# Quantising the first layer's weights ahead of the feed-forward block, and turning its inputs by DMA

## What is computed

```python
# x: 8 x 512 x 1024, context: 8 x 512 x 1024, 64 heads of 8 rows, L = 1024
kv  = einsum('bhil,bhjl->bijhl', ctx, ctx)             # per head 8 x 8 products
out = causal_convolution(kv, ssm_kernel) + kv * D      # along l, for each head
out = einsum('bijhl,bhil->bjhl', out, layernorm(x))
x   = x + tanh(g_xattn) * out                          # the "mixer"
h = bf16(layernorm_weighted(bf16(layernorm(x))))
h = bf16(mx_quant(h) @ mx_quant(W1).T + b1)            # W1: 4096 x 1024
h = bf16(gelu_tanh(h))
h = bf16(mx_quant(h) @ mx_quant(W2).T + b2)            # W2: 1024 x 4096
x = x + tanh(g_ffn) * bf16(residual + h)
# mx_quant: blocks of 32 along the contraction share the power of two of their largest magnitude;
# values are rounded to integers on that scale and clipped to -128..127
```

## Time and profile before

| | |
|---|---|
| median of three runs | 2044.43 us |
| the profiled execution itself | 2045.5 us |
| its span in the trace | 2043.7 us |
| PE busy | 1931.1 us (94%) |
| DVE busy | 1735.5 us (85%) |
| POOL busy | 967.6 us (47%, nearly all of it in the mixer) |
| ACT busy | 735.7 us (36%) |

### The profile page before, as it was taken

The page is one execution under the profiler, slowest core; times in us unless marked ns, Lnnn a source line. Parts: engine busy times, 40 slices in busy tenths (PEclk is TensorE's granted clock), DMA queues, the critical chain, the costliest instruction groups (busy, mean ns, idle before and its releaser), DMA issues. The chain is left out here.

```text
span 2043.7 us, 29510 instructions
## 1 busy us (share of the span) xinstructions
PE 1931.1 (94%) x11776; PEld 1488.6 (73%) x11776; DVE 1735.5 (85%) x2092; ACT 735.7 (36%) x1028; POOL 967.6 (47%) x1036
## 2 busy tenths in 40 slices
PE   6999999999999999999826599999999999999998
PEld 5888888888788888888725466677776666667763
DVE  6888898898899999999779979888888888888843
ACT  3232222222222222222126444545544444455540
POOL 3888888888899999999912000000000000000000
PEclk9999999999999999999958799999999999999999
DMA  6555555555354555544437401111111111111111
GB/s 220 188 201 195 195 192 195 196 200 211 127 181 175 182 174 177 190 165 168 164 124 278 166 31 51 43 63 63 63 63 63 42 52 63 63 42 52 42 42 73
DMA packets 65769, 264.40 MB, mean 129 GB/s; under 512 B 7712, under 2 KB 7712, under 8 KB 57440
## 3 DMA queue, kind: packets, MB, share of 16 engines
q1 hardware_dynamic: 65632, 262.52, 36.1%
HBM read 219.96 MB, written 42.53 MB: 128 GB/s over the span
## 5 line engine op out<-in xcount | busy, mean ns | idle before, releaser
L242 PE MATMUL y_ps<-kk_hi,slab 128*128 128x512 f32 (+8 forms) x3072 | 872.9, 367 | 9.3 <-DMA slab<-taps_scratch 5.2
L242 PEld LDWEIGHTS y_ps<-kk_hi,slab 128*128 128x128 f32 x3072 | 559.2, 189 | 106.3 <-DMA slab<-taps_scratch 5.6
L242 PE MATMUL y_ps<-kk_lo,slab 128*128 128x512 f32 (+8 forms) x1536 | 563.0, 367 | 0.0
L714 PE MATMUL l_ps<-f_xq_T,w_T 128*128 128x256 bf16 x4096 | 461.4, 276 | 16.3 <-ACT arena L793 13.6
L714 PEld LDWEIGHTS l_ps<-f_xq_T,w_T 128*128 128x128 bf16 x4096 | 404.7, 99 | 70.3 <-ACT arena L793 13.9
L729 PE MATMUL acc_ps<-w_T,arena 128*128 128x512 bf16 x2048 | 449.0, 379 | 0.0
L729 PEld LDWEIGHTS acc_ps<-w_T,arena 128*128 128x128 bf16 x2048 | 199.2, 98 | 231.8
L1059 POOL TENSOR_TENSOR f_rstd<-f_var_eps,f_neg_half 128x1 f32<-128x1 f32 x32 | 23.4, 733 | 716.0 <-DVE f_var_eps L857 716.0
L242 PEld LDWEIGHTS y_ps<-kk_lo,slab 128*128 128x128 f32 x1536 | 290.5, 189 | 47.9
L793 ACT ACTIVATE arena<-l_ps,f_b 128x256 bf16<-128x256 f32 x512 | 214.3, 473 | 221.1 <-PE l_ps L714 215.3
L508 POOL TENSOR_TENSOR lsum<-lower 128x240 f32<-128x240 f32 (+1 forms) x128 | 252.5, 1973 | 73.4 <-DVE lower L384 73.4
(11 more groups left out here) (109 smaller groups left out, 1901.1 us busy)
## 6 DMA issues: line engine op xcount, KB each, us to landing
slab<-taps_scratch SPq DMA_DIRECT2D x128, 512.0 KB, 4.4
arena<-in_w_m SPq DMA_DIRECT2D x32, 1024.0 KB, 6.6
arena<-x_scratch SPq DMA_DIRECT2D x64, 512.0 KB, 4.2
k_ext<-in_ctx_e SPq DMA_DIRECT2D x64, 384.0 KB, 3.0
arena<-in_w SPq DMA_DIRECT2D x24, 1024.0 KB, 6.5
x_tile<-in_x_t SPq DMA_DIRECT2D x32, 512.0 KB, 4.5
x_scratch<-x SPq DMA_DIRECT2D x32, 512.0 KB, 2.9
out_t<-arena SPq DMA_DIRECT2D x32, 512.0 KB, 2.6
```

The source lines that it names most:

```text
L242: mm = nc.tensor.matmul(y_ps[:, y_base + begin:y_base + end], slab[s][:, half, d * P:(d + 1) * P], kk_part[s][:, begin - d * PAIR:end - d ...
L714: mm = nc.tensor.matmul(l1_ps[bank % L1_BANKS][:, a, :], w1_T[:, k, col:col + P], xq_T[:, k, :], start=(k == 0), stop=(k == L // P - 1))
```

## The change

In the mixer all 32 raw tiles (W1 and W2) have their maxima taken in heads 0 to 20, two in an even head and one in an odd one; the scales follow in head 20. Four buffers of 1 MB replace two and two. From head 21 on three tiles are quantised per four heads, first the 16 of W2, then the 16 of W1, which now comes from the host in transposed layout. As a block of 32 of W1 then runs over partitions, its inverse scales must be spread over partitions: ACT repeats them (`repeat_inverses`), PE multiplies by a bf16 identity into `turn_ps` (`spread_inverses`, in heads 22, 24, 26 and 28), and ACT copies the result (`keep_inverses`). All 32 quantised tiles go to scratch memory. In the feed-forward block W1's work on DVE, PE and ACT is gone; both layers' weights are plain loads. The inputs are turned by a transposing DMA from SP's queue into `xq_T`, two per group, in place of PE's transposes and ACT's copies; PSUM gives layer 1 a fourth bank.

The diff, cut to what the text speaks of:

```diff
-L1_BANKS = 3
+L1_BANKS = 4
 # mixer, plan over heads
+    maxima_heads = 2 * (2 * W_TILES) // 3
+    scales_head = maxima_heads - 1
+    quant_head = maxima_heads
+    spread_heads = [quant_head + quant_head % 2 + 2 * i for i in range(4)]
+    for n in range(2 * W_TILES):
+        maxima_of[n // 3 * 2 + (n % 3 == 2)].append(n)
+    for n in range(2 * W_TILES):
+        ints_of[quant_head + (4 * n + 1) // 3].append(n)
+        quant_of[min(quant_head + (4 * n + 3) // 3, heads - 1)].append(n)
 # mixer, SP, per head
-                if 1 <= h < tiles - 1:
-                    sp.wait_ge(w_max_ready, h)
-                    load_w(h + 1)
...
+                if h >= 1:
+                    for n in maxima_of[h - 1]:
+                        load_w(n + W_SLOTS)
+                    for n in quant_of[h - 1]:
+                        store_w(n)
 # mixer, PE, after stretch 1 of heads 22, 24, 26, 28
+            def spread_inverses(r):
...
+                for n in range(LB):
+                    mm = nc.tensor.matmul(turn_ps[:, n, :], inv_rows[:, n * P:(n + 1) * P], ident_bf[:], start=True, stop=True)
 # mixer, DVE, one W1 tile
+                    nc.vector.tensor_tensor(w_int.rearrange("p (k o) -> p k o", o=2 * P),
+                                            w_raw[raw % W_SLOTS].rearrange("p (k o) -> p k o", o=2 * P),
+                                            view(inv_T, j * 2 * P, [(0, LB), (1, 2 * P)]), ALU.mult).then_inc(w_ints, 1)
+                    nc.vector.tensor_scalar(w1_scale.bitcast(U16), inv_T[:, j * 2 * P:(j + 1) * 2 * P].bitcast(U16),
+                                            -1.0, 254.0 * 128, ALU.mult, ALU.add).then_inc(w1_scaled, 1)
 # feed-forward, SP
+            def turn_input(t):
+                s, g = t % GROUP, t // GROUP
+                sp.wait_ge(x_quant, t + 1)
+                if g >= 1:
+                    sp.wait_ge(l1_ready, banks * g)
+                sp.dma_start(xq_T[:, :, s * P:(s + 1) * P], hq[s][:], transpose=True).then_inc(input_turned[s], 16)
...
+            for j in range(3):
+                load_layer1(j)
+            for t in range(GROUP, 2 * GROUP):
+                load_tile(t)
+            turn_input(0)
+            for j in range(3, 6):
+                load_layer1(j)
+            turn_input(1)
+            for j in range(6, W_TILES):
+                load_layer1(j)
+            for j in range(W_TILES):
                 load_layer2(j)
...
                 if 1 <= g <= groups:
                     store(GROUP * (g - 1))
                     reload(GROUP * (g - 1) + 1)
+                for s in range(GROUP):
+                    if g + 1 < groups:
+                        turn_input(GROUP * (g + 1) + s)
 # feed-forward, PE
                 if b == 0:
-                    pe.wait_ge(input_kept, GROUP * (g + 1))
+                    for done in input_turned:
+                        pe.wait_ge(done, 16 * (g + 1))
-            for j in range(n1):
-                turn_weights(j)
-                if j >= 1:
-                    layer1(0, j - 1)
...
-                        if s == 0 and g + 1 < groups:
-                            turn_input(GROUP * (g + 1) + part)
 # feed-forward, DVE: weight_ints, weight_clip, weight_quant are removed
```

More of the change, by code:

```diff
@@ L35 @@
 X_SLOTS = 4
-W_BUFS = 4
+W_SLOTS = 4
+W_TILES = 16
 GROUP = 2
@@ L191, in _ @@
                 load_x(t)
-            load_w(0)
-            load_w(1)
+            for n in range(W_SLOTS):
+                load_w(n)
             for h in range(heads):
@@ L205, in _ @@
                         load_x(t + 3)
[L206 to L215 removed]
+                if h >= 2:
+                    for n in quant_of[h - 2]:
+                        if n + W_SLOTS < 2 * W_TILES:
+                            load_w(2 * W_TILES + n + W_SLOTS)
+                if h >= 1:
[3 more added lines that the diff above has]
+                        store_w(n)
             for parity in range(2):
@@ L218, in _ @@
             first_loads(sp)
-            store_w2(tiles - half - 1)
+            for n in quant_of[heads - 1]:
+                store_w(n)
             store_x1(tiles - 1)
-            sp.wait_ge(w2_stored, 16 * (tiles - half))
+            for stored in w_stored:
+                sp.wait_ge(stored, 16 * (2 * W_TILES // W_SLOTS))
             for parity in range(2):
@@ L466, in _ @@
                     low_half(h + 1)
-                if h < tiles:
-                    weight_maxima(h)
-                if h == tiles:
+                for n in maxima_of[h]:
+                    weight_maxima(n)
+                if h == scales_head:
                     weight_scales()
[L471 to L476, removed]
+                for n in range(2 * W_TILES):
+                    if n in ints_of[h]:
+                        weight_ints(n)
+                    if n in quant_of[h]:
+                        weight_quant(n)
             times_q(heads - 1, 1)
@@ L832, in _ @@
                     norm_again(GROUP * (g - 1))
-                for s in range(GROUP):
-                    if g + 1 < groups:
-                        keep_input(GROUP * (g + 1) + s)
                 for s in range(GROUP):
@@ L1003, in _ @@
                 quantise_input(t)
-            weight_quant(0)
-            for j in range(1, n1):
-                weight_ints(j)
-                if j >= 2:
-                    weight_quant(j - 1)
-                weight_clip(j)
-                if j in (6, 7):
-                    first_statistics(j - 4)
-                if j in (11, 12):
-                    second_statistics(j - 9)
-                if j in (9, 13):
-                    peak(0, (j - 9) // 4)
-            weight_quant(n1 - 1)
+            for t in range(GROUP, 2 * GROUP):
+                first_statistics(t)
             for g in range(groups + 2):
                 for s in range(GROUP):
-                    if 1 <= g and g + 1 < groups:
+                    if g + 1 < groups:
                         second_statistics(GROUP * (g + 1) + s)
```

277 lines of the change are left out of this document (115 added, 162 removed).

## The result

After the change the kernel takes **2136.2 us** (median of 4 runs, 2134.3 to 2139.2); before it took 2044.5 on the same chip (4 runs, 2044.0 to 2045.0). The ratio is 1.045, 95% interval 1.0437 to 1.0463: slower, by 92 us. The forecast was 2115.

A forecast was written before the change was run, and what follows sets the result against it. PE was taken to bound the mixer, narrowly over DVE, and the feed-forward steady state; 2045.5 + 23 (mixer) - 55.6 (first groups) + 103 (steady state) = 2115.9, less 1.1 for the median: 2115 us, range 2030 to 2200.

The forecast's parts named there:

- The steady state: Feed-forward block: PE waits for transposes queued behind store and reload, 14 groups of 6.2 - 1.36 + 2.5 us, +103.
- T: Steady state: time from the first transposing DMA's issue until both have landed and layer 1 starts, taken as 6.2 us.
- The clock: Steady state: PE's clock falls after idling before layer 1, taken as 2.5 us per group.
- Rival A: Steady state: transposes land like a plain store in 2.6 us, no clock loss, 2029 us as a median; chance 0.17.
- Rival B: Steady state: a transposed byte costs four plain ones, both transposes take 13 us, 2210 us in all; chance 0.16.
- The first groups: Feed-forward block's start to the end of layer 1 of group 1: 103.3 us against 158.9 before, -55.6.
- The mixer: Heads from 21 on: quantising more tiles makes PE wait for DVE, +23 us, bounds +10 to +45.
- below 30.91: no cost: Mixer, heads 0 to 20: three maxima per two heads bring DVE to 29.7 us, under PE's 30.91, so nothing lost.
- DVE needs 31.7 us per two heads, and PE waits 0.8 of them: Mixer from head 21: 1.5 tiles quantised per two heads; for W2's 11 pairs this costs 9 us.
- The 0.5: Mixer, W1 part: assumed us for the extra 256-column operation per W1 tile, between nothing and the clip's 1.20.
- Rival C: Mixer: POOL and DVE block each other, PE's clock falls, 45 us lost instead of 23, 2137 in all; chance 0.12.
- Zero terms: Mixer: spreads on PE and ACT, and added SP and DMA traffic, are hidden; spreads about 4 us without PE slack.

The follow-up runs named there:

- turn_first: The kernel after the change, with SP issuing the next group's two transposing DMAs ahead of the store and the reload: 2037.1 us, ratio 0.9963.
- pe_warm: The kernel after the change, with 48 dummy matmuls on PE after layer 2 in groups 1 to 14: 2116.7 us, ratio 1.0354.
- halves: The kernel after the change, with the maxima taken in half tiles, three halves in each of the first 21 heads: 2129.9 us, ratio 1.0416.
- pool_light: The kernel after the change, with most of POOL's sums in the mixer left out: 2100.7 us, ratio 1.0277.
- w1_out: The kernel after the change, with VectorE's multiplication and clip of W1 left out except 32 columns: 2099.7 us, ratio 1.0276.

## Why the prediction was right, and where it was off

The sign and the time came out: 2136 lies in the range of 2030 to 2200, in the forecast's own range of 2075 to 2165 too, and it is 21 above the 2115. Of the profiled execution (2134.3 against 2115.9) the three terms, mixer, first groups and steady state, were off by +37, -4 and -15. That the total came so near is in part luck: the errors of the other two took back half of the mixer's.

**The steady state, forecast +103, measured +87.6.** The mechanism is as put: the transposes stand behind the reload, which waits for the store; PE idles from the end of layer 2 and its clock falls. T, first issue to layer 1, was put at 6.2 and is 1350.98 - 1345.39 = 5.6. The clock was put at 2.5 and took 1.4 to 2.7 (29.49 to 30.83 against 28.11), 2.1 on average. A usual group so costs 6.6 us more instead of 7.3, and the last group's layer 1 waits only 1.86 us and runs at full clock (28.11). The usual period of 63.1 lies inside 62 to 66. `turn_first` shows the list to be the whole cause, `pe_warm` the clock's part of it. Rival A, T as a plain store, did not hold in this place; the nearest row, 1024 KB in 6.5 us, was closer. Rival B, four times the price of a plain byte, fell too: with nothing else on the queue a transpose of 256 KB lands in 3.1 to 3.2 us (`turn_first`, least and median), the second one after 1.27 us more of issue, which makes an estimated 4.5 for both. The rest of the 5.6 comes with the reload in front. So "as fast as regular DMAs", the rule of the Trainium skill (Advanced Engine Details and Errata, X-Bar Transpose), is not far off for the transfer; near a tie came out wrong with it, since it counts neither the time of the two issues nor the reload. And the 1309 ns that the Trainium skill (VectorE: DVE Perf Modes, The three transpose paths) has for one block can't be added up: the eight blocks of one transpose would take an estimated 10.5 us, and they landed in 3.2.

**The first groups, forecast -55.6, measured -59.5.** The block needed 99.4 us where 103.3 were forecast (and 158.8 before, not 158.9): the second tile and its transpose were 1.4 us quicker (layer 1 starts 24.9 into the block against 26.3), layer 1 of group 0 took 29.45 where I had 29.95, and layer 1 of group 1 ends 45.0 after group 0's, against 47. Here the transposes did wait as long as in rival B, though for another reason: two issues took SP 11.37 us (at 1147.55) right behind the bulk of W2's loads. The wait for ACT's `first_norm` and first bias covered them: the fifth bank started 23.9 us after the end of layer 1 of group 0, where 24.1 were forecast.

**The mixer, forecast +23, measured +60.4.** This is the term that was mis-sized, and the step that failed is "below 30.91: no cost" and, behind it, "DVE needs 31.7 us per two heads, and PE waits 0.8 of them". VectorE's need was right to 0.3 us: 30.0 for the maxima (29.7 forecast), 31.6 for W2 (31.7), 32.7 for W1 (32.4). What was wrong was to read the pair's length straight from the sum. Runs and trace share it out, in part by estimate:
- *Maxima*, ten pairs, +7: VectorE had 5% of idle time, and PE still waited, since two maxima in one head overran what fits. `halves` took just this away.
- *W2*, ten pairs from 375.30 to 701.88, 32.66 against 31.7 forecast, +10 on the term: the sum of 31.6, 2% for the pauses between its operations that the busiest windows have too (31.6 / 0.98 = 32.2, an estimate), and some 0.4 left for the peaks. It was wrong to give the engine 100%.
- *W1*, ten pairs from 701.88 to 1043.56, 34.17 against 32.4, +18: as W2, plus the scale operation at 0.85 us instead of 0.5 (0.5 a pair), and the clock, 0.98 in the window where waits of up to 2.4 us stand. The 0.5 was near the 0.44 that it takes in `pool_light`; what the sum had left out is its wait for POOL.
- The stall at head 20 was 5.8, not 7.07, -1; the remaining 3 or 4 are not traced; the two microseconds that I let VectorE's idle time at the start hide may be among them.

**Rival C** had the right time, 2137, by a route that was only half right. That the mixer gives way by more than 23 was its claim, and POOL and VectorE do block each other (`pool_light`, `w1_out`). But its sign, `times_q` waiting for POOL's sums, is nowhere in the trace; the blocking is inside VectorE's own durations. The rows of before had most of it already: 2790, 1925 and 1196 ns, where `pool_light` has 2396, 1327 and 846. The prediction saw that POOL is slower beside the quantisation and did not ask what VectorE loses by the same block. Only `kk_lo` had been free of it, 2565 ns before and 2776 after. C's 45 were too few still, and its total of 2137 was reached with the steady state at 103.

**Zero terms.** Spreads, SP's list and the DMA traffic in the mixer were put at nothing, and rightly: `w1_out` runs W1's part at 30.9 with all of its traffic, and heads with spreads take no longer than those without (130.45 and 130.71 us for eight).

## What to carry to other kernels

- When work moves from an engine's program into a DMA queue, its place in that queue is part of the change: a transfer that feeds the busiest engine belongs ahead of anything that waits for a store to land.
- A second engine that comes within some 5% of the bound can already be on the path, if its work is uneven. Don't count on more than 98% of it, the most seen here, and ask for each turn of the loop, not on average, how much extra work fits before the bound engine's next need. Cut extra work into equal shares, but expect little from this where the sum is near the bound.
- When one engine's rows are longer beside another's work, look for the same in the other engine's rows, and price new operations with it.
- An idle gap of some 5 us on TensorE costs about 2 us more behind it, at the lower clock.

## What the runs showed of the hardware

- One SBUF-to-SBUF transpose of 128x1024 bf16 takes SP 1.23 us to issue at the least and 1.6 at the median, where the plain DMAs next to it take 0.3 to 0.7. It lands in 3.1 to 3.2 us when alone, and in up to 12.5 in the whole kernel, with the first groups' bulk loads. SP's issue times of it (min, median, max in ns) and its landing in the kernel after:

```profile
L699 SPq DMA_TRANSPOSE f_xq_T<-f_hq x32: 1231/1616/8189, 1107.8 to 2038.3; - x32
...
DMA to landing us min/median/max: 3.1/4.4/12.5
```

- POOL's additions lengthen VectorE's operations with two SBUF inputs by 0.23 to 0.49 us each, the clip with one SBUF input by 0.14 (986 against 846 ns), and leave alone those that read PSUM and SBUF.
- A small operation can last as long as POOL's: the one on 128x256 uint16 that makes W1's scales takes 854 ns in the kernel after, 436 in `pool_light` and 214 in `w1_out`, and a clip of only 32 columns took 0.98 us in `w1_out`.
